# Where the reciprocal square roots of two layer norms run: VectorE in place of GpSimd

## The reference

```python
def _layernorm(x, axis=-1, eps=1e-05):
    m = jnp.mean(x, axis=axis, keepdims=True)
    v = jnp.var(x, axis=axis, keepdims=True)
    return (x - m) / jnp.sqrt(v + eps)

# x: (16, 112, 512); ctx: (16, 375, 512); mask: (16, 112, 375); 16 heads of 32
x = x + xattn(_layernorm(x), ctx, mask, wq, bq, wk, bk, wv, bv, wo, bo)
#   q = w8a8_linear(xn, wq, bq)      rows and weights rounded to 8-bit levels
#   k = ctx @ wk.T + bk;  v = ctx @ wv.T + bv
#   o = softmax(q k^T / sqrt(32) + mask) v  per head;  w8a8_linear(o, wo, bo)
x = x + ffn(_layernorm(x), W1, B1, W2, B2)
#   rows and weights rounded to 8-bit levels, 512 -> 2048, gelu, 2048 -> 512
```

## Time and profile before

| | us |
|---|---|
| median of 3 runs | 915.63 |
| lowest and highest run | 914.07, 920.92 |
| span of the profiled execution, first to last instruction | 912.3 |

### The profile page before, as it was taken

The page is one execution under the profiler, slowest core; times in us unless marked ns, Lnnn a source line. Parts: engine busy times, 40 slices in busy tenths (PEclk is TensorE's granted clock), DMA queues, the critical chain, the costliest instruction groups (busy, mean ns, idle before and its releaser), DMA issues.

```text
span 912.3 us, 17970 instructions
## 1 busy us (share of the span) xinstructions
PE 749.9 (82%) x5424; PEld 588.2 (64%) x5424; DVE 616.2 (68%) x1353; ACT 457.7 (50%) x1117; POOL 264.9 (29%) x474
## 2 busy tenths in 40 slices
PE   0387779899897989898998989798989899896734
PEld 0275658687675868576877767586857687674512
DVE  4767557675867767675867676786757586856543
ACT  2314446556565647464555656564746455564500
POOL 0303022331514232413324151423242432411111
PEclk9785779979799979999899979997999989998855
DMA  9339772434344443434344434343343434352000
GB/s 326 126 106 278 251 175 77 109 96 110 96 120 106 116 105 87 105 93 104 91 98 114 109 94 118 104 118 95 91 104 92 110 93 98 89 118 55 11 0 10
DMA packets 85325, 100.27 MB, mean 110 GB/s; under 512 B 34144, under 2 KB 72800, under 8 KB 84656
## 3 DMA queue, kind: packets, MB, share of 16 engines
q1 hardware_dynamic: 85280, 99.72, 41.3%
HBM read 51.71 MB, written 11.01 MB: 69 GB/s over the span
## 4 chain that ended last, share of the span: by engine, by line
PE 57%; DVE 20%; issue 8%; POOL 7%; DMA 3%; ACT 2%; SPq 2%; POOLq 1%; DVEq 0%; ACTq 0%
PE ps_proj L944 20%; PE ps_t L987 8%; PE ps_m L1042 7%; PE ps_m L1061 6%; PE ps_o L1000 5%; DVE cols L855 4%; PE ps_s L979 3%; DVE h_q L735 3%; PE ps_proj L928 2%; PE ps_m L1053 2%; POOL ctx_lo L518 2%; POOL x_nw L495 2%; DVE h L849 2%; SPq L414 2%; POOL x_rs L496 2%
## 5 line engine op out<-in xcount | busy, mean ns | idle before, releaser
L612 ACT ACTIVATE probs<-probs,neg_max 112x375 f32<-112x375 f32 x256 | 155.4, 607 | 182.1 <-DVE neg_max L777 181.7
L777 DVE CUSTOM_DVE_ANT_0 probs<-ps_s,mask_in 112x375 f32<-112x375 f32 x256 | 135.1, 545 | 87.4 <-PE ps_s L979 77.8
L987 PE MATMUL ps_t<-ident,probs 112*125 112x112 f32 x768 | 150.8, 313 | 11.8 <-ACT probs L612 6.9
L987 PEld LDWEIGHTS ps_t<-ident,probs 112*125 112x125 f32 x768 | 130.7, 217 | 39.7 <-ACT probs L612 25.6
L979 PE MATMUL ps_s<-k_stack,q_stack 96*112 96x376 f32 x256 | 107.3, 446 | 44.8 <-DVE neg_max L777 42.7
L621 ACT ACTIVATE pT<-ps_t 125x336 f32<-125x336 f32 x256 | 113.2, 442 | 20.2 <-PE ps_t L987 18.9
L518 POOL TENSOR_TENSOR ctx_lo<-ctx_in,ctx_hi 128x376 fp32r<-128x376 f32 x64 | 64.2, 1013 | 198.0 <-ACT ctx_hi L577 194.4
L502 POOL TENSOR_SCALAR h<-h,cols 112x1024 f32<-112x1024 f32 x16 | 26.4, 1652 | 235.4 <-DVE cols L862 160.5
L944 PE MATMUL ps_proj<-ctx_hi,wk_hi 128*128 128x376 f32 x256 | 92.5, 361 | 0.7 <-ACT q_scale L583 0.7
L979 PEld LDWEIGHTS ps_s<-k_stack,q_stack 96*112 96x112 f32 x256 | 47.4, 199 | 62.7 <-DVE neg_max L777 55.7
L944 PE MATMUL ps_proj<-ctx_lo,wk_hi 128*128 128x376 f32 x256 | 87.1, 340 | 0.0
(11 more groups left out here) (125 smaller groups left out, 1401.7 us busy)
## 6 DMA issues: line engine op xcount, KB each, us to landing
k_stack<-k_hi SPq DMA_DIRECT2D x256, 94.0 KB, 2.2
k_stack<-k_lo SPq DMA_DIRECT2D x128, 94.0 KB, 2.2
ctx_in<-in_ctxT SPq DMA_DIRECT2D x32, 375.0 KB, 3.5
q_stack<-q_dram SPq DMA_DIRECT2D x48, 224.0 KB, 4.3
h<-in_w2T SPq DMA_DIRECT2D x4, 1024.0 KB, 6.2
b_row<-in_w2T SPq DMA_DIRECT2D x4, 1024.0 KB, 7.0
x_in<-in_x SPq DMA_DIRECT2D x16, 224.0 KB, 2.6
q_dram<-q_hi SPq DMA_DIRECT2D x16, 224.0 KB, 2.0
```

The costliest lines, as they stand in the source:

```text
L612: nc.scalar.activation(probs[:, hd % SP_RING, :], probs[:, hd % SP_RING, :], ACT.Exp, scale=-1.0, bias=neg_max[:, par, hd:hd + 1], accum_o ...
L777: nc.vector.tensor_tensor_reduce(out=probs[:, hd % SP_RING, :], in0=ps_s[hd % 2][0:N, 0:L], in1=mask_in[:], scale=-1.0, scalar=BIG, op0=AL ...
L987: last = nc.tensor.transpose(ps_t[hd % 2][0:LR, lc * N:(lc + 1) * N], probs[:, hd % SP_RING, lc * LR:(lc + 1) * LR], ident[0:N, 0:N])
```

## The change

The function `rsqrt` and its two callers go from GpSimd's program to VectorE's. It is the same nine instructions with the same waits and the same `settle`. On VectorE the x chain runs directly behind `bn_aggr` of `x_norm`, the y chain directly behind `bn_aggr` of `y_norm`. The units `x_norm` and `y_norm` are gone from `POOL_UNITS`; VectorE's table is unchanged. GpSimd no longer waits for the previous sample's `x_norm_s` and `y_norm_s` before it starts a chain; on VectorE program order holds that.

```diff
 POOL_UNITS = (
-    ("residual", 0), ("split", 0), ("split", 1), ("x_norm", 0), ("split", 2), ("x_quant", 0), ("split", 3), ("y_norm", 0),
+    ("residual", 0), ("split", 0), ("split", 1), ("split", 2), ("x_quant", 0), ("split", 3),
     ("prepare", 4), ("y_quant", 0), ("h_quant", 0),
 )
...
+            def rsqrt(b, mv, rs, nw, chain):
+
+                n = [0]
+
+                def link(ins):
+                    n[0] += 1
+                    ins.then_inc(chain, 1)
+                    dve.wait_ge(chain, NEWTON_LINKS * b + n[0])
+                    settle(dve)
+
+                link(nc.vector.tensor_scalar(nw[:, 0:1], mv[:, 1:2], EPS_LN, 1.0, ALU.add, ALU.mult))
+                link(nc.vector.tensor_scalar(rs[:].bitcast(I32), nw[:, 0:1].bitcast(I32), -0.5, RSQRT_SEED, ALU.mult, ALU.add))
+                link(nc.vector.tensor_scalar(nw[:, 0:1], nw[:, 0:1], -0.5, 1.0, ALU.mult, ALU.mult))
+                for step in range(NEWTON):
+                    link(nc.vector.tensor_scalar(nw[:, 1:2], rs[:], rs[:], nw[:, 0:1], ALU.mult, ALU.mult))
+                    link(nc.vector.tensor_scalar(rs[:], nw[:, 1:2], 1.5, rs[:], ALU.add, ALU.mult))
...
                 nc.vector.bn_aggr(x_mv[:], x_st[:]).then_inc(x_mean, 1)
+                dve.wait_ge(x_mean, b + 1)
+                settle(dve)
+                rsqrt(b, x_mv, x_rs, x_nw, x_newton)
...
                 nc.vector.bn_aggr(y_mv[:], y_st[:]).then_inc(y_mean, 1)
+                dve.wait_ge(y_mean, b + 1)
+                settle(dve)
+                rsqrt(b, y_mv, y_rs, y_nw, y_newton)
```

More of the change, by code:

```diff
@@ L479, in prepare @@
                                                    bass.bass_isa.ReduceOp.max).then_inc(w_max, 1)
[L481 to L496, removed]
             def round_rows(b, rows, r, quant, chain, done, scale_done):
@@ L505, in round_rows @@
                 nc.gpsimd.tensor_scalar(quant, rows, -ROUND, 1.0, ALU.add, ALU.mult).then_inc(done, 1)
[L507 to L512, removed]
             def split_lo(b, par, i):
@@ L532, in residual @@
                 nc.gpsimd.tensor_tensor(xres[:], xres[:], bo_row[:], ALU.add).then_inc(xres_s, 1)
[L534 to L539, removed]
             def y_quant(b, par, i):
@@ L550, in _ @@
             pool.wait_ge(c_in, 16 * 5)
-            units = {"prepare": prepare, "x_norm": x_norm, "split": split_lo, "x_quant": x_quant, "residual": residual,
-                     "y_norm": y_norm, "y_quant": y_quant, "h_quant": h_quant}
+            units = {"prepare": prepare, "split": split_lo, "x_quant": x_quant, "residual": residual,
+                     "y_quant": y_quant, "h_quant": h_quant}
             slots(pool, lambda *a: run(POOL_UNITS, units, *a))
```

## The result

The changed kernel takes **985.82 us** (median of 4 runs, 982.95 to 992.97) where the kernel before takes 917.79 in the same comparison (914.07 to 920.92): ratio **1.075**, 95% interval 1.0696 to 1.0804. The forecast was 952, with a range up to 976. The direction was right, and the loss is nearly twice as large. The profiled execution after took 992.97 us with a span of 991.2, so 78.9 us more span than before. It is the slowest of the four, and 1.8 us lie outside its span as outside every other one listed, so the profiled execution before, with its span of 912.3, must be the one of 914.07, the fastest. That is why the profiles differ by 78.9 us and the medians by 68.0.

The account below looks back on a forecast made before the run. PE was taken to set most of the time, DVE some stretches of a slot. Y chain +34.2, x chain -3.9 and ends +6.6 gave +36.9 us on a 912.3 span, 952 us with 3.3 around it; range 928 to 976.

Parts of the forecast that it names:

- PE has no idle time in which to catch up: Slots 1 to 14, behind transpose 7: q and all behind it stay late by the y chain's mean 2.44 us.
- The idle time hides the rest: Ahead of head 0, slots 2 to 14: the x chain delays head 0 by only 0.93 us.
- The price of one chain: On DVE behind `bn_aggr`: 1.93 us of links plus 1.5 of gaps, less 0.12, pushes everything behind by 3.3 us.
- gaps of 0.03 us: Rival: gaps between links on DVE as small as without `settle`, a push of 2.1 us, 926 us; chance 0.12.
- The y chain, 2.44 us a slot: Slots 1 to 14: the push of head 6 delays `k_hi`, transpose 7 and q; +34.2 us in all.
- The x chain, -0.30 us a slot: Slots 2 to 14: +0.93 for head 0, -0.59 for the `x_rs` wait, -0.64 for L791; -3.9 us in all.
- The relief of the addition: L791, slots 2 to 14: pushed behind GpSimd's first two splits, it falls to about 0.69 us, -0.64 a slot.
- The clock falls as well: Rival: behind the y chain's hole 3 us of PE work at half speed lose 1.5 us a slot, 973 us; chance 0.17.
- PE still has S 8, S 9 and PV 0 in the hole: Argument against the clock falling: PE keeps this work in the hole ahead of transposes 6 and 7.
- The ends, +6.6 us: Slots -1, 0, 1, 15 and 16 for +2.15, +1.1, 3.3, +0.9 and -0.9 us.
- The 3.3 us that the sum put around the span: Time outside the profiled span, added to the forecast span of 949.2 us to give 952.

Follow-up runs that it names:

- two Newton steps: Changed kernel with VectorE's loop written out and two Newton steps instead of three in both chains; 942.08 us, 1.0248 to 1.0319 of the kernel before.
- y's chain alone: Against the kernel before, only the y chain moves to VectorE and x's stays on GpSimd, with the loop kept; 961.42 us, ratio 1.0449 to 1.0511.
- the kernel written out and filled: Changed kernel with VectorE's slots 3 to 12 written out instead of looped, and eight unneeded matmuls behind k 0; 956.97 us.
- x alone with the loop written out: Kernel before with only x's chain moved to VectorE and VectorE's loop written out; 918.18 us, ratio 1.0013 to 1.0046.
- x from sample 3: Kernel before with VectorE's loop written out and x's chain on VectorE only from sample 3, y's on GpSimd; 913.28 us, ratio 0.9972.
- y's chain, written out and filled: Kernel before with only y's chain moved to VectorE, VectorE's loop written out and eight unneeded matmuls behind k 0; 952.65 us.
- before written out: Kernel before, both chains still on GpSimd, with only VectorE's loop written out, as a control; 920.51 us, ratio 1.0037 to 1.0093.
- the eight matmuls: Unneeded matmuls added behind k 0 on TensorE; in the changed kernel 971.96 us with the loop, 956.97 with it written out.
- the kernel written out: Changed kernel, both chains on VectorE, with VectorE's program for slots 3 to 12 written out instead of looped; 990.16 us.

## Why the prediction was right and wrong

The measured 986 us lie above the range. Two steps of the prediction failed, each a term that the sum had at nothing. "PE has no idle time in which to catch up" counted PE's work behind the y chain at its old speed; it ran at half the clock for 6.8 us, which costs 2.95 us in each slot where it happens. "The idle time hides the rest", of the x chain, took no account of the loop's turn, whose stall takes that idle time first. The terms that the sum did have came out near.

*The price of one chain: right, a little small.* Links of 154, 214 and 273 ns for 153, 214 and 275; gaps of 0.15 us. Only the last gap, to the next head, is longer, 0.33 to 0.76 us where I took 0.15. So from `y_mv` to head 6 it is 3.6 to 4.0 us, a push of 3.5 to 3.9 for my 3.3. The gaps inside the chain bear out the 0.15 us. That it is the increment which makes them is read from rows with and without one; no run takes it out of the chain, so whether a chain with gaps of 0.03 us was to be had stays open. The Trainium skill, page "VectorE: DVE Perf Modes", section "The DRAIN you can't avoid", says that a semaphore after each of eight copies costs nothing over one after the last. Here, with a wait and an increment between dependent links, the gap is 0.15 us each time, and the measurement decides; gaps of 0.03 us would have given 926 us. The addition of `bv_row` takes 691 or 692 ns on average in every run with all nine links of x's chain on VectorE from the start, 869 with two Newton steps, which push it less far, and 1179 with y's chain alone, where it stands beside the splits as before. That agrees with the Trainium skill, page "SBUF — State Buffer", section "SBUF: two separate sides", on the two engines' lock.

*The y chain, 2.44 us a slot: right.* 2.0 to 2.6 measured; that one pair gives 2.41 is partly luck. The path is that of the forecast. In slot 7 of the kernel written out and filled `k_hi` starts 5.50 us behind `y_mv` (468.42, 462.92) and transpose 7 starts 6.71 behind it, released by ScalarE; before it was 2.98 and 4.19. Both move by 2.52 us, where the forecast had 2.25 for this slot and 2.63 for the next. But PE's first wait is one that the sum didn't have, that of head 8's scores.

*The x chain, -0.30 us a slot: right in a kernel without turns.* x alone with the loop written out has 49.07 us a slot, 0.51 less than before; x from sample 3 0.45 less. Beside y's chain, written out and filled, it is 0.34 less (51.65 against 51.99), and beside before written out 0.94. Part of it may be the clock: before, slots with a mean clock of 0.97 take 49.2 us and those with 0.90 take 49.8, while with x alone written out all have 0.93 and 49.0 to 49.4. The two halves of the term were both too small: head 0 comes 4.68 us behind `x_st` instead of 3.40, +1.28 for my +0.93, and y's statistics follow head 0 after 11.52 us instead of 12.94 to 13.27, -1.4 to -1.8 for my -1.23. The relief of the addition (L791 at 1213 ns, now 692) is as forecast. "The idle time hides the rest" was the step that failed in the loop: at every turn the stall takes that idle time first.

*Missed altogether: the turn of VectorE's loop.* I costed each instruction of the chains, and never the length of the loop's body that they stand in. Against slots at the same low clock its stall costs 2.7 us in each of four slots, 11 us, and with the eight matmuls the turns cost 15.0; without them the gain in the next slots pays it back. The trace of before has no such stall, so no row of it could give the price; but a change that adds instructions to a loop should have had a rival for it.

*"The clock falls as well": the rival with 0.17 was the case.* It had the right mechanism, the right place and 1.5 us a slot. Measured it is 2.95 us where it strikes: PE idles 2.26 us, and then 6.8 us, not 3, run at a granted clock of 0.50. "PE still has S 8, S 9 and PV 0 in the hole" was wrong: S 8 is what waits, for the bank of `ps_s` that head 6's maximum frees, and the others stand behind it. The forecast itself took "PE has no idle time in which to catch up" and stopped there; PE's work at half speed was the other half of it.

*The ends, +6.6 us: too small.* Slots -1 and 0 gave +5.0 for 3.25; slot 1 +7.7 for 5.7, with a clock of 0.84 behind its y; slot 16 about -1.2 for -0.9. From x's statistics of slot 14 to y's of slot 15 it was +5.5, and from there to y's of slot 16 +5.3, for 2.1 and 0.9. With the loop written out the second has only +0.8, so its term was right; the other 4.5 us go with PE at half clock in two stretches of its densest work, as these windows of the changed kernel show:

```profile
912.00:922.00 10.00, 9.12 (x50) 6.11 (x51) 5.71 (x18) 4.07 (x12) 1.27 (x1) 0.50 0.01 2
...
932.00:942.00 10.00, 9.31 (x59) 6.48 (x60) 3.25 (x6) 3.11 (x9) 3.52 (x3) 0.51 0.01 2
```

In the kernel written out the clock is back at 0.97 between 12 and 16 us behind y's statistics of slot 15, where it is 0.50 here. Why it comes back earlier there is open. The 3.3 us that the sum put around the span were 1.8.

**The sum as the runs give it**, for the profiled span of +78.9: slots 2 to 13 +24.8 for both chains (51.65 - 49.58, twelve times; forecast 25.7), about +11 for four turns, about +20 for the low clock (six slots at 0.69 and one at 0.84); the ends and slots 1 and 14 +22.4 (forecast 11.2), of which some 9 are the clock (1.6 in slot 1, 3.0 in slot 14, 4.5 in slot 15, by the same stretches of the filled and, for slot 15, of the written-out kernel). The forecast described the change at full clock and without the turns; both chains in that form take 956.97 us.

## What to carry to other kernels

A row of small dependent instructions put ahead of work that another engine waits for costs its whole length each time round, and the idle time that is to hide it can be spent once only: look for what else will claim it, a loop's turn among them. When such a push opens an idle time of 2 us on TensorE ahead of its densest stretch, price the work behind it at half the clock too: here it was 6.8 us of work and 2.95 us a slot, where I had allowed for 3 and 1.5. Where a change makes a loop's body longer, try it with the loop written out before judging it: here that took x's chain from 2.2% slower to 0.3%.

## What the runs showed of the hardware

- VectorE stands still for 2.2 to 3.6 us at the turn of its loop when the body is longer by 18 or 36 links of a chain or by 112 increments a turn; in the kernel before there is none, and none where the loop is written out. With x's chain alone it is 3.3 to 3.6 us, with y's alone 2.2 to 2.5, with both 2.3 to 2.4, which I can't explain.
- Behind a stall of 2.3 us in every second slot TensorE's mean clock behind y was 1.00 (slots of 52.0 us), and without the stall every slot had 0.69 (54.5). The stall removed gave nothing back by itself, and 15 us once eight matmuls kept the clock up.
- Eight needless matmuls of 128x376 a slot made the kernel 33 us faster with VectorE's loop written out (990.16 to 956.97) and 14 us with the loop (985.82 to 971.96).
- `tensor_scalar` on 112x1 costs 154 ns with constants, 214 ns with one column as scalar and 273 ns with two.
